# A graph attention layer on one core: a GpSimd memset between the fourth and the fifth gather of each pair

## The reference

```python
q = (x @ Wq + bq).reshape(N, H, D)
k = (x @ Wk + bk).reshape(N, H, D)
v = (x @ Wv + bv).reshape(N, H, D)
e = (edge_attr @ We).reshape(-1, H, D)
alpha = einsum('ehd,ehd->eh', q[dst], k[src] + e) / sqrt(D)
a = exp(alpha - segment_max(alpha, dst)[dst])
attn = a / segment_sum(a, dst)[dst]
out = segment_sum(attn[:, :, None] * (v[src] + e), dst).reshape(N, 128)
x_r = x @ Wskip + bskip
beta = sigmoid(concat([out, x_r, out - x_r]) @ Wbeta)
out = layernorm(beta * x_r + (1 - beta) * out) * gamma + beta_ln
return layernorm(x + (x + relu(out)))
```

## Time and profile before

| | us |
|---|---|
| median of three timed runs | 2459.15 |
| lowest, highest | 2456.94, 2463.15 |
| the profiled execution | 2454.78 |
| its span, first to last instruction | 2453.0 |
| GpSimd busy in the span | 1492.3 (61%) |
| TensorE busy (matmul) | 1762.1 (72%) |
| VectorE busy | 1720.9 (70%) |
| mean granted TensorE clock | 0.824 of full speed |

### The profile page before, as it was taken

How to read it: one execution, slowest core, us unless ns; L and a number is a source line. 1 busy time by engine, 2 the same in 40 slices (tenths; PEclk the granted TensorE clock), 3 DMA queues, 4 the chain that set the end, 5 groups by cost and what they waited for, 6 DMA issues and landing times. The chain is left out here.

```text
span 2453.0 us, 35080 instructions
## 1 busy us (share of the span) xinstructions
PE 1762.1 (72%) x10434; PEld 1597.7 (65%) x10434; DVE 1720.9 (70%) x2897; ACT 805.9 (33%) x1889; POOL 1492.3 (61%) x1580
## 2 busy tenths in 40 slices
PE   7667777777777777777777776777767776767773
PEld 5566766766666666666667665676667666667662
DVE  6566665666666666677677777777777777777886
ACT  0122222222322332333333333333343334334446
POOL 0466666666666666666666666666666666666650
PEclk9788888888887888888887889879887888887885
DMA  8755656656555555555655555555566566656641
GB/s 302 243 186 185 198 179 201 193 181 199 184 166 171 167 185 169 171 182 163 186 176 167 188 173 178 179 174 186 171 198 191 183 196 191 194 178 200 198 144 48
DMA packets 231807, 449.01 MB, mean 183 GB/s; under 512 B 42082, under 2 KB 151752, under 8 KB 218974
## 3 DMA queue, kind: packets, MB, share of 16 engines
q1 hardware_dynamic: 156304, 241.36, 30.1%
q0 software_dynamic: 75312, 205.36, 27.9%
HBM read 404.57 MB, written 41.99 MB: 182 GB/s over the span
## 5 line engine op out<-in xcount | busy, mean ns | idle before, releaser
L784 POOL DMA_INDIRECT kv<-kv_tab,src_all x1498 | 1421.8, 949 | 706.7 <-issue 409.7
L1020 PE MATMUL sum_ps<-wv,hot_en 128*128 128x136 f32 x3136 | 563.7, 309 | 367.5 <-issue 345.7
L1020 PEld LDWEIGHTS sum_ps<-wv,hot_en 128*128 128x128 f32 x3136 | 464.7, 209 | 420.2 <-issue 413.3
L908 PE MATMUL q_all<-q_win,hot_ne 128*128 128x128 f32 x3136 | 452.5, 306 | 3.2 <-DVE prod L1505 1.9
L908 PEld LDWEIGHTS q_all<-q_win,hot_ne 128*128 128x128 f32 x3136 | 443.6, 225 | 7.0 <-issue 6.2
L1505 DVE TENSOR_TENSOR prod<-q_all,kve 128x1024 f32<-128x1024 f32 x196 | 240.0, 1225 | 288.4 <-remote 273.6
L1494 DVE TENSOR_TENSOR kve<-kv,e_ps 128x768 f32<-128x768 f32 (+1 forms) x392 | 407.4, 1080 | 7.1 <-issue 5.3
L1168 ACT ACTIVATE wt_ps<-logit,used_b 128x64 f32<-128x64 f32 x196 | 62.2, 318 | 1061.1 <-issue 862.5
L893 PE MATMUL e_ps<-we,tab_buf 128*128 128x128 f32 x1568 | 307.2, 361 | 112.2 <-issue 88.1
L893 PEld LDWEIGHTS e_ps<-we,tab_buf 128*128 128x128 f32 x1568 | 282.7, 268 | 141.4 <-issue 134.0
L893 PE MATMUL e_ps<-we,ea 128*128 128x128 f32 x1568 | 318.6, 377 | 72.9 <-issue 51.8
(11 more groups left out here) (151 smaller groups left out, 1096.1 us busy)
## 6 DMA issues: line engine op xcount, KB each, us to landing
ea<-eaT SPq DMA_DIRECT2D x49, 1024.0 KB
row_b<-rel_row SPq DMA_DIRECT2D x98, 512.0 KB
tab_buf<-eaT SPq DMA_DIRECT2D x49, 1024.0 KB
kv<-kv_tab,src_all POOLq DMA_INDIRECT x1498
q_win<-q_tab SPq DMA_DIRECT2D x252, 64.0 KB
sum_tab<-sums SPq DMA_DIRECT2D x251, 59.5 KB
kv_tab<-tab_buf SPq DMA_DIRECT2D x33, 384.0 KB, 3.9
logit<-sum_tab SPq DMA_DIRECT2D x49, 136.0 KB
```

The source lines that it names most:

```text
L784: pool.indirect_dma_start(out=head_rows(q) if u == t == 0 else kv[:, s, t, :], out_offset=None, in_=kv_tab[:, :], in_offset=bass.IndirectO ...
L908: mm = pe.matmul(q_ps[u][:, t * P:(t + 1) * P], hot_ne[:, 2 * par + u, t * P:(t + 1) * P], q_win[:, 2 * par + min(u, parts(q) - 1), :], st ...
L1020: mm = pe.matmul(sum_ps[1 if wide else u][:, 0:AC], hot_en[:, 2 * par + u, t, :], wv[:, 2 * par + u, t, :], start=(t == 0 and not (wide an ...
```

## The change

GpSimd gets a scratch row `rest` of one partition and 700 float32 numbers, and a semaphore `rest_ok`. Between the fourth and the fifth gather of each pair (after the wait of the fifth gather, before the gather itself) it sets the row to zero and counts up the semaphore. From the second pair on it waits before that for the memset of the pair before. Nothing reads the row.

```diff
+REST = 700
...
+        rest = sb("rest", [1, REST])
...
+        rest_ok = sem("rest_ok")
...
                         tile = (2 * q + u) * TILES_G + t
                         if tile >= REAL_TILES:
                             continue
+                        if u == 1 and t == 0:
+                            if q:
+                                pool.wait_ge(rest_ok, q)
+                            pool.memset(rest[:, :], 0.0).then_inc(rest_ok, 1)
                         pool.indirect_dma_start(
```

## The result

Nine timed runs of each kernel on the chip of the first profiles: 2458.72 us before (2456.38 to 2463.15), 2469.0 us after (2462.75 to 2480.33). The ratio is 1.0046, with a 95% interval from 1.003 to 1.0062. The medians are 10.3 us apart, more than the 0.3% that the prediction called measurable. The runs of after also spread over 18 us, those of before over 7.

A forecast was written before the change was run, and what follows sets the result against it. The pace was taken to be TensorE's side of the loop, near 11.76 us a pair. 192 pairs x 0 + 0.9 us on the profiled 2454.8 gave 2455.7, thus 2460.0 for the median; range 2446 to 2478.

The forecast's parts named there:

- A: The memset between gathers four and five is absorbed in GpSimd's stand; 2460.0 us, by itself 2450 to 2470; chance 0.74.
- F: A small drift: VectorE is held for part of the 0.68 us in late pairs, +12 us, 2472; chance 0.02.
- The memset's own time: The memset of 700 float32 on one partition takes 681 ns, from the slope between two memset rows.
- What it adds: Memset plus issue between gathers four and five adds 0.9 us a pair to GpSimd, bounds 0.38 and 0.98.
- the 1.1 to 1.4 that I named: Sign of a right forecast: the stand before head gathers falls from 2.03 to 1.1 to 1.4 us.
- The wait on rest_ok: GpSimd's wait for the memset of the pair before, 11.8 us older, is met at once; cost zero.
- The start: In pair 0 VectorE waits for gathers 5 to 8, now 0.9 us later: +0.9 us once.
- The margin of 1.73 us: GpSimd's idle time before each pair's head gather, 2.03 less 0.30 us of issue, covers the added work.
- Rival B: Added cost between gathers four and five passes 1.73 us, GpSimd becomes the bound: 2549 or 3690 us; chance 0.09.
- the gathers have no part in the late release: q_ok's late release at the heads isn't due to gathers, by the group at 1935.27 and the empty stretch at 112.7.
- Rival C: TensorE's release hangs on the last gather, so every pair grows by the memset's cost: +173 us, 2632; chance 0.07.
- rival D: The mid-group pause spreads the gathers' traffic and TensorE's cycle shortens by 0.1 us: -19 us, 2441; chance 0.06.

## Why the prediction was right in its size, and where it was not

**The number.** 2460.0 forecast, 2469.0 measured, inside 2446 to 2478. But the likeliest case, A, said no measurable change, and the interval of 1.003 to 1.0062 lies above that. The outcome has the sign and size of F (+12 us), which had 0.02, and not F's mechanism. On the third chip A's "within 0.3%" holds (1.0011). On the second only parts and variants of the change were run, at 0.9991 to 1.0014. That 2469.0 lies inside the range on the first chip is in part luck: the margin that carried the forecast is there, for a reason that the prediction had wrong.

**The memset's own time: right.** 681 ns from two rows, 671 measured, and 671 to 674 in all 195.

**What it adds: mis-sized.** 0.9 us taken, 0.53 measured, inside the bounds of 0.38 and 0.98. The 0.9 stood near the upper end since gathers always show their 0.30 us; the memset starts without it and the gather behind it needs 0.16. The stand fell to 1.53 us, above the 1.1 to 1.4 that I named. The wait on rest_ok was free, as said: the memset starts at the end of the gather.

**The start: wrong, and small.** +0.9 us was expected where VectorE waits for gathers of pair 0. That wait is 1.38 us in after instead of 1.79, and the product behind it starts 0.14 us earlier (95.61, 95.75 in before). The head of pair 4 is earlier too.

**The margin of 1.73 us: right in its use, wrong in what it is.** In the usual pairs of the first and the third chip 0.53 us went into the stand and cost 0.01 to 0.02 us. Rival B's threshold holds as well: three clears, 1.98 us, make GpSimd the bound. But the step before it failed: that the gathers have no part in the late release. Two rows carried it. The group with 0.34 us more of issue and an unchanged interval shows that a short delay is absorbed, not that gathers are innocent. The stretch with DMA at zero shows a release that comes 4 us after a group that had followed another without a stand. That is the pattern of the irregular places, so it speaks as much for a part of the gathers, some microseconds later, as against it. I had marked the release 7.4 us after the matmuls as strange and went on. It was the main fact: the same kernel without gathers 5 to 8 takes 0.767 of the time. One label is off without effect: the gathers issued from 1006.45 us are those of pair q+1, not q+2, and it is they that VectorE reads at 1023.38.

**Rival C (the release hangs on the gathers, 0.07): half right.** Its mechanism is in the trace, TensorE held while gathers are issued, and its price of +173 us is not. On the first chip VectorE's product, which waits for the same q_ok, came a median 1.87 us after the last gather's issue in before and 1.37 us in after. So the release does not come a fixed time after the last gather. It may be that what counts is how much time without gathers TensorE finds in a pair, 2.03 us of stand before and 1.53 + 0.53 us after. But these medians can't show it: with an interval that stays the same, this sum stays the same by arithmetic, and a release that comes a fixed 11.5 us after the head (median 11.50 and 11.53) fits them too. Only the three clears speak for it, since there the release moved from a median 11.65 to 8.06 us after the head (before and three clears, third chip). That is also the mechanism of rival D, a pause that lets TensorE's cycle run ahead, with GpSimd paying more for the pause than the cycle gains.

**Rival B (0.09): is the truth of the fourth chip**, with a margin of nothing and not by the paths that I gave it. The memset never waited for VectorE. Most of VectorE's operations beside it don't test this, since one of their two inputs lies in PSUM (e_ps, q_all, wt_ps). L1629 has both in SBUF (`u_xt` and `u_bent`, parts of the `logit` buffer), and in the run with the clear before the second gather it is under way when a memset starts:

```profile
1937.92 0.42 DVE L1629 SCALAR_TENSOR_TENSOR logit<-logit 128x256 f32<-128x256 f32 x1
1937.94 0.67 POOL L790 MEMSET rest<- 1x700 f32 x1
```

The memset starts at the end of the gather before it and takes its 0.67 us, and L1629 takes 0.42 us as elsewhere. Of the two pages of the Trainium skill that stood against each other, "GPSIMD Engine Reference" (Key points, contention with operations of two SBUF inputs) is not borne out for a memset, and the narrower list of "SBUF — State Buffer", which names GpSimd operations that read SBUF, is in agreement with it. In the traces of the fourth chip 5 of 781 clears took longer than 680 ns, the longest 727, with no cause shown; that is 0.06 us at most and not rival B's 1.22. Nor was code loaded: no clear of after has an idle time of microseconds before it.

**What stays open.** What inside the chip holds TensorE's matmuls and signals while gathers are issued and for some 2 us after the last one, in the earlier trace rows even with the DMA engines at zero, and what then sets the pace of 11.76 to 11.92 us. Why one chip of four doesn't do it, with the same kernel; each set ran once on its chip, so chip and set aren't told apart. Whether two clears would make the kernel faster where TensorE is held: GpSimd's list then asks for 11.26 us a pair, less than the 11.92 of the third chip, but that run fell on the chip that doesn't hold it. Why the irregular places that the clear brings lie in early pairs, and why the first chip has 14 and the third one. That these places make the loss on the first chip is read from its trace, since no run took them away there.

## What to carry to other kernels

A stand says how much work fits only after you know what ends it: here the 2 us of stand at each head came from a signal that TensorE gave late, on three chips, and didn't exist on the fourth, where 0.52 us a pair in two other places cost 4.8%. Idle time of an engine that is put down to "issue", hundreds of microseconds ahead of one line of matmuls, and a semaphore that comes 6.5 us after the matmul that raises it, are rows to follow before any other: between a chip that holds TensorE and one that doesn't lie 379 us, and the change was worth 10. When the spread of the runs grows with the median (18 us against 7), look for a few irregular places before you divide the loss by the number of pairs.

## What the runs showed of the hardware that I had not expected

- The same kernel took 2458.7, 2486.6, 2491.2 and 2111.8 us in the four sets, the last three on three chips by number, each within 0.3% of its own median. The traces put the difference to TensorE: 410 us of idle time without a wait ahead of one line on the third chip, none put down to issue there in the run with the clear before the second gather on the fourth.
- Held and not held, the same 3136 matmuls of that line have a mean of 312 and 283 ns, and the mean granted clock of the kernel before on the third chip is 0.814 against 0.96 without gathers 5 to 8. A low clock is not what the idle times need: from 111 to 114 us TensorE idles 2.08 and 1.14 us between matmuls at a granted clock of 1.00.
- A pause of 2.3 us in GpSimd's stream of gathers brings the median delay of q_ok from 6.5 to 0.48 us and TensorE's idle time ahead of its sums from 410 to 62 us, although GpSimd has next to no stand otherwise.
- A one-partition memset of 700 floats costs GpSimd 0.52 to 0.53 us between two gathers (0.67 + 0.16 - 0.30), the next ones 0.73 us each.
